# Smaller steps for GpSimd in a two-layer cross-attention kernel: weight pieces in three, a bias sum in four, stores issued later

## The chip, the core and the metric

The kernel runs on one core of one Trainium2 chip. The core has five engines that work side by side, each through its own list of instructions in order: TensorE (PE, matrix products), VectorE (DVE), ScalarE (ACT), GpSimd (POOL) and SyncE (SP, which here only issues transfers). They wait for one another through semaphores. The metric is the time of one execution on the device in microseconds (us); the median of three runs is compared.

## What is computed

Two layers of cross-attention with 16 heads of 32, all in float32. Shapes: `x` and `ctx` are 8 x 512 x 512.

```python
def L0(tgt, memory):                 # attention without a norm
    q, k, v = heads(tgt @ Wq.T), heads(memory @ Wk.T), heads(memory @ Wv.T)
    att = softmax(q @ k.T / sqrt(32)) @ v
    return tgt + att[0]              # batch 0's result is added to every batch
def L1(x, y):
    xq, ykv = layer_norm(x, gq, bq), layer_norm(y, gkv, bkv)
    q, (k, v) = heads(xq @ Wq), heads(ykv @ Wkv)
    x = x + softmax(q @ k.T * SCALE) @ v @ Wproj + bproj
    h = gelu(layer_norm(x, gm, bm) @ W1 + b1)      # 512 to 2048
    return x + h @ W2 + b2                         # 2048 to 512
```

Only `att[0]` is used, so layer 0 is worked for batch 0 alone; layer 1 for all eight batches.

## The kernel before

To keep float32 accuracy on PE, every operand is split into a rounded high part and the low rest, and a product is made of three matmuls (high x high, high x low, low x high). Making the parts is the work of ACT (high) and of DVE or POOL (low).

**Ticks.** A planner writes the order of all engines before the run. Its unit is a tick: in one tick PE makes one block of scores (128 queries x 512 keys of one head, `ps_s`, line 901), the transposed block for the softmax of seven ticks earlier (`ps_t`, 916), and the product with the values of nine ticks earlier (`ps_o`, 883), so this product follows its `ps_t` by two ticks. Between them stand parts of projections and of the MLP (`ps_d`, 862, with transposes at 792). A head is four ticks, a batch 64. The planner runs layer 0's batch first (ticks 6 to 78), then layer 1's eight batches (from tick 87), one behind the other; the MLP of batch n is worked beside the attention of the batch after it, and that of batch 8 in a tail of its own (from tick 608). Each engine goes through the ticks in the same order and does in each what the tables list for it; it waits on semaphores only, so POOL runs ahead where its inputs are there.

**What POOL does in a tick**, in this order: `p_lo` of two blocks in four (line 1285; the other two are DVE's, 1188), the joins of a group of four heads (`join`, 1256 to 1273), the norm's four small instructions (`var_e` to `shift`, 1243 to 1249), the low part of the GELU (`g_s`, 1293), low parts of whole weights, then a weight piece, an X sum (layer 0's result added to a batch of `x`, 1306), a residual sum (1320), and the bias sum. The `p_lo` of a block is needed by PE two ticks later; PE waits for it with everything behind it.

**Weight pieces.** `W1` and `W2` are split once, in 16 pieces (0 to 7 are `W1`, 8 to 15 `W2`), and written back to DRAM as high and low parts, from where the MLP loads them. `piece(i)` on POOL casts a loaded piece (`w_raw` to `piece_out`, 128 x 1024) and subtracts. Pieces 0 to 7 start at ticks 25, 30, ... 60, with load and store on SP's queue; 8 to 15 at ticks 91, 96, ... 126, on ACT's queue. The load is issued three ticks before the piece, the store two ticks (SP) or four (ACT) after. Two buffers alternate, so piece i waits until the store of piece i - 2 has landed.

**The bias sum.** After the layer norm of batch n has read `xres` (ACT, line 991), POOL adds `b2` to it, one instruction of 128 x 2048 (line 1325), at ticks 175 for batch 1, 239, 303, 367, 431, 495, 559 for batches 2 to 7, and 613 for batch 8. The MLP's second product adds to `xres` afterwards (DVE, 1119), some 30 ticks later, in the tail three ticks later. From batch 2 on, the same tick is one in which ACT makes the GELU of the batch before it in one burst, and in each of the four ticks behind it POOL has one `g_s`.

**SyncE's queue.** It issues in order the loads of heads (`q_st`, `k_st`, 707), the load of the row of maxima that each `ps_t` needs (`negmax_t`, 712), and the placing of finished heads (723, 724). The first head of a group waits until POOL's join of the group before has ended (`o_joined`, wait at 720), with all that stands behind it on the queue.

Of the kernel before, what the change touches and what calls it, by code (L numbers as in the profile page):

```python
# [5 lines left out]
F32 = mybir.dt.float32  # L6
F32R = mybir.dt.float32r
ACT = mybir.ActivationFunctionType
ALU = mybir.AluOpType
AX = mybir.AxisListType  # L10

P = 128
T = 512
D = 512
# [5 lines left out]
TC = T // P  # L20
HC = F // P
G = P // DK
# [7 lines left out]
NP = B + 1  # L30
# [191 lines left out]
def listed(pairs):  # L222
    out = {}
    for t, x in pairs:
        out.setdefault(t, []).append(x)
    return out
# [11 lines left out]
NORM_NO = {u: i for i, u in enumerate(NORMS)}  # L238
# [18 lines left out]
def ready(*u):  # L257
    return NO[u] + 1
# [8 lines left out]
def norm_ticks(kind, i):  # L267

    if kind == "y" or i and kind == "x":
        at = PLAN.end("a", (2 if kind == "y" else 10) + i, 0) - 6  # L270
        if i == 0:
            at = PRE + 1
        elif (kind, i) == ("x", 1):
            at = PLAN.gap + 3
        return (at, at, at + 1, at + 1), at + 2, (at + 3, at + 3, at + 4, at + 4)
    if kind == "x":
        at = PLAN.gap + 2
        return (at,) * 4, at, (at + 1,) * 4
    at = tuple(emptied("out", i, t) for t in range(TC))
    return at, at[-1], (at[-1] + 1,) * 4  # L280
# [46 lines left out]
PIECES = 16  # L327


def piece_tick(i):  # L330
    return PRE + 19 + 5 * i if i < PIECES // 2 else PLAN.base[1] + 4 + 5 * (i - PIECES // 2)


PIECE_SPLIT = listed([(piece_tick(i), i) for i in range(PIECES)])
X_SUMS = listed([(norm_ticks("x", b)[0][0] - (4 if b > 2 else 3) + t if b > 1 else PLAN.gap + 3, (b, t)) for b in range(1, B) for t in range(TC)])
RES_SUMS = listed([(PLAN.base[n + 1] + (4 if n == 1 else 3) + t, (n, t)) for n in range(1, NP) for t in range(TC)])
BIAS_AT = PLAN.base[2] + 2
WO_AT = PLAN.base[1] + 48
B2_SUMS = listed([(norm_ticks("h", n)[2][0] + 1, n) for n in range(1, NP)])


def sync_tables():
# [79 lines left out]
def xattn_program(nc, x, ctx, l0wq, l0wk, l0wv, wq, wk, wv, wo, w1, w2, cols, bproj, b2, ident, out):  # L422
# [179 lines left out]
    def piece_view(i, a):  # L602

        if i < PIECES // 2:
            return piece_out[:, i % 2].rearrange("p c (k a j) -> p c k a j", k=FC, a=2)[:, :, :, a]
        return piece_out[:, i % 2].rearrange("p c (a j) -> p c a j", a=2)[:, :, a]

    def piece_in(i):
        if i < PIECES // 2:
            return w1_raw[:, i % 2].rearrange("p c (k j) -> p c k j", k=FC)  # L610
        return w2_raw[:, i % 2]
# [40 lines left out]
    def load_piece(queue, i):  # L652
        if i < 2:
            queue.wait_ge(whole_split, len(WHOLE))
        elif i in (PIECES // 2, PIECES // 2 + 1):
            queue.wait_ge(unit_ready, ready("a", 10, FC - 1))
        else:
            queue.wait_ge(piece_split, i - 1)
        src = w1 if i < PIECES // 2 else w2
        c = 2 * (i % (PIECES // 2))  # L660
        queue.dma_start((w1_raw if i < PIECES // 2 else w2_raw)[:, i % 2], src[c:c + 2].rearrange("c p e -> p c e"))\
            .then_inc(piece_loaded[i % 2], 16)

    def store_piece(queue, i):
        queue.wait_ge(piece_split, i + 1)
        dst = w1d if i < PIECES // 2 else w2d
        c = 2 * (i % (PIECES // 2))
        queue.dma_start(dst[c:c + 2].rearrange("c p e -> p c e"), piece_out[:, i % 2].bitcast(F32))\
            .then_inc(piece_stored[i % 2], 16)
# [15 lines left out]
        queue.dma_start(rows(out, n - 1)[:, t], xres[n % 2][:, t]).then_inc(out_stored[n % 2], 16)  # L685

    def load_wo(queue):
        queue.wait_ge(piece_split, PIECES)
        queue.dma_start(wo_raw[:], wo).then_inc(wo_loaded, 16)


# [2 lines left out]
    def _(sp):  # L694
# [58 lines left out]
        for tick in range(TICKS):  # L753
            for h in ROWS.get(tick, []):
                load_row(h)
            early = tick < SHARED_FROM
            for u in STORES.get(tick, []) if early else ():
                store(sp, *u)
            for h in HEADS.get(tick, []):
                load_stack(h)  # L760
            for h in PLACES.get(tick, []):
                place_head(h)
            for n, g in VALUES.get(tick, []) if early else ():
                load_values(sp, n, g)
            for kind, j in LATE_W_LOADS.get(tick, []):
                load_weight(kind, j)
            for n, t in OUT_STORES.get(tick, []):
                if n == NP - 1:
                    store_out(sp, n, t)
            for kind, b in STAGE_LOADS.get(tick, []) if early else ():  # L770
                load_stage(sp, kind, b)
            if tick == PRE:
                load_stage(sp, "y", 1)
            for name, at in WHOLE_LOAD.items():
                if tick == at:
                    load_whole(name)
            for i in range(PIECES // 2):
                if tick == piece_tick(i) - 3:
                    load_piece(sp, i)
                if tick == piece_tick(i) + 2:  # L780
                    store_piece(sp, i)
        last = NP - 1
        sp.wait_ge(out_stored[last % 2], 16 * TC * (last // 2))
# [144 lines left out]
    def _(act):  # L928
# [71 lines left out]
        for tick in range(TICKS):  # L1000
# [52 lines left out]
            for i in range(PIECES // 2, PIECES):  # L1053
                if tick == piece_tick(i) - 3:
                    load_piece(act, i)
                if tick == piece_tick(i) + 4:
                    store_piece(act, i)
            if tick == WO_AT - 4:
                load_wo(act)
# [17 lines left out]
    def _(dve):  # L1077
# [4 lines left out]
        def evacuate(kind, n, c):  # L1082
            u = (kind, n, c)
            if kind == "a":
                low(u, aT[:, n % 2, 1, c], aT[:, n % 2, 0, c])
            elif kind == "ht":
                low(u, hT[:, 1, c], hT[:, 0, c])
            elif kind in ("k", "q"):
                j = KQ_NO[u] % 2
                low(u, kq_out[:, j, 1], kq_out[:, j, 0])  # L1090
            elif kind == "v":
                j = V_NO[u] % 2
                low(u, v_out[:, j, :, 1:2 * DK:2], v_out[:, j, :, 0:2 * DK:2],
                    lambda b: b.rearrange("p (h d) -> p h d", h=NH))
            elif kind == "tg":
                dve.wait_ge(unit_ready, NO[u] + 1)
                if c == 0:
                    dve.wait_ge(piece_split, PIECES // 2)
                added, own = bank(u).rearrange("p (t d) -> p t d", t=TC), slice(c * P, c * P + P)
                dve.tensor_copy(tgt2[:, :, own], added)  # L1100
                dve.tensor_tensor(xt0[:, :, own], xt0[:, :, own], added, ALU.add).then_inc(evacuated, 1)
            elif kind == "out":
                if c == 0:
                    dve.wait_ge(res_summed, n)
                dve.wait_ge(unit_ready, NO[u] + 1)
                dve.tensor_tensor(xres[n % 2][:, c], bank(u), xres[n % 2][:, c], ALU.add).then_inc(evacuated, 1)
            elif kind == "hid":
                done = GELU_NO[n, c // 4]
                if done:
                    dve.wait_ge(g_lo, 4 * done - 3 + c % 4)  # L1110
                dve.wait_ge(unit_ready, NO[u] + 1)
                dve.tensor_scalar(h_st[:, c % 4], bank(u), col_s[:, 6 * FC + c:6 * FC + c + 1], None,  # L1112
                                  ALU.add).then_inc(evacuated, 1)
            else:
                if c < TC:
                    dve.wait_ge(b2_summed, n)
                dve.wait_ge(unit_ready, NO[u] + 1)
                t = c % TC
                dve.tensor_tensor(xres[n % 2][:, t], bank(u), xres[n % 2][:, t], ALU.add).then_inc(evacuated, 1)
# [86 lines left out]
    def _(pool):  # L1206
# [5 lines left out]
            if c == FC - 1:  # L1212
                ins.then_inc(whole_split, 1)

        def piece(i):
            if i == 0:
                pool.wait_ge(unit_ready, ready("k", 0, G - 1))
            if i >= 2:
                pool.wait_ge(piece_stored[i % 2], 16 * (i // 2))
            pool.wait_ge(piece_loaded[i % 2], 16 * (i // 2 + 1))  # L1220
            pool.tensor_copy(piece_view(i, 0), piece_in(i)).then_inc(piece_hi, 1)
            pool.wait_ge(piece_hi, i + 1)
            pool.tensor_tensor(piece_view(i, 1), piece_in(i), piece_view(i, 0).bitcast(F32), ALU.subtract)\
                .then_inc(piece_split, 1)

        def split_wo(c):
            if c == 0:
# [50 lines left out]
        for tick in range(TICKS):  # L1278
# [15 lines left out]
                                   ALU.subtract).then_inc(g_lo, 1)  # L1294
            for name, c in WHOLE_LO.get(tick, []):
                whole_low(name, c)
            for i in PIECE_SPLIT.get(tick, []):
                piece(i)
            for b, t in X_SUMS.get(tick, []):
                i = STAGE_NO["x", b]  # L1300
                buf = stage[:, i % 2]
# [12 lines left out]
            for n, t in RES_SUMS.get(tick, []):  # L1314
# [5 lines left out]
                ins = pool.tensor_tensor(xres[n % 2][:, t], xres[n % 2][:, t], tgt2[:, t], ALU.add)  # L1320
                if t == TC - 1:
                    ins.then_inc(res_summed, 1)
            for n in B2_SUMS.get(tick, []):
                pool.wait_ge(normed, NORM_NO["h", n] + 1)
                pool.tensor_tensor(xres[n % 2][:], xres[n % 2][:], b2_s[:].unsqueeze(1).broadcast_to([P, TC, D]),
                                   ALU.add).then_inc(b2_summed, 1)
            for c in range(FC):
                if tick == WO_AT + 2 * c:
                    split_wo(c)
# [45 lines left out]
```

## Time and profile before

| | |
|---|---|
| median of three runs | 1836.07 us (1834.27 to 1836.93) |
| span of the profiled execution | 1833.4 us; its time outside the span is not listed |
| PE busy | 1730.2 us, 94% |
| ACT, DVE, POOL busy | 63%, 59%, 51% |
| mean granted PE clock | 0.982 of full speed |
| DMA | 354.69 MB, mean 193 GB/s |

The profile is of one execution, with times in us from the span's start. "Busy" is the time in which an engine works on an instruction; an engine can be busy half of the time and still be late where it matters. Where a row carries brackets, they hold the idle time of that engine just before the instruction and who ended it. The span and the median differ by 2.67 us, which is of the size of what is between the runs.

### The profile page before, as it was taken

To read this page: it belongs to the slowest core of one execution; us is meant where nothing else is said; L and a number is where in the kernel's file an instruction comes from. 1 tells how busy PE (TensorE), PEld (TensorE's weight loads), DVE (VectorE), ACT (ScalarE), POOL (GpSimd) and SP (SyncE) were. 2 spreads that over 40 slices of the span, in tenths; PEclk is the share of its full clock that TensorE was granted. 3 is DMA by queue.
4 is the path that set the end of the run, shared out by engine and by line. 5 is a ranking of instruction groups with operands and counts; after the bars stand their busy time and mean duration, and the time that the engine had idled before them with its cause. 6 is when DMAs were issued, how large, how long until landed. Compare 5 with 4: busy or idle time off the path is not lost.

```text
span 1833.4 us, 23939 instructions
## 1 busy us (share of the span) xinstructions
PE 1730.2 (94%) x7488; PEld 1328.0 (72%) x7488; DVE 1082.3 (59%) x1860; ACT 1156.9 (63%) x1935; POOL 933.7 (51%) x778
## 2 busy tenths in 40 slices
PE   6899998987899899999999999999999999999898
PEld 5677776765666677777777767777777777777686
DVE  4566664576776566666666665666666666564322
ACT  3677774587877675766766676667667665774231
POOL 0355531287874465466555554655556445555331
PEclk8999999999999999999999999999999999999999
DMA  6688954897645664576577556756755765567262
GB/s 233 217 295 276 301 210 153 266 319 248 209 130 166 169 196 117 167 227 181 153 216 199 139 155 188 200 130 194 231 156 159 200 189 146 162 198 243 94 215 92
DMA packets 157102, 354.69 MB, mean 193 GB/s; under 512 B 29232, under 2 KB 47792, under 8 KB 156080
## 3 DMA queue, kind: packets, MB, share of 16 engines
q1 hardware_dynamic: 101744, 174.63, 32.3%
q10 hardware_dynamic: 55232, 178.53, 30.3%
q8 instruction: 61, 1.00, 0.2%
q14 instruction: 65, 0.53, 0.1%
HBM read 251.51 MB, written 82.08 MB: 182 GB/s over the span
## 4 chain that ended last, share of the span: by engine, by line
PE 65%; ACT 10%; DVE 7%; POOL 6%; DMA 5%; issue 5%; SPq 1%; ACTq 1%; DVEq 1%; POOLq 0%
PE ps_d L862 43%; PE ps_o L883 11%; PE ps_t L916 5%; PE ps_s L901 5%; DMA q_st<-negmax_t 3%; DVE negmax L1175 1%; POOL p_lo L1285 1%; ACT p_hi L1015 1%; ACT ps_d L936 1%; POOL stage L1306 1%; ACT ps_t L1022 1%; ACT ht L991 1%; DVE stats L1132 1%; PE ps_d L792 1%; ACT h_st L1006 1%
## 5 line engine op out<-in xcount | busy, mean ns | idle before, releaser
L1285 POOL TENSOR_TENSOR p_lo<-p_full,p_hi 128x512 fp32r<-128x512 f32 x288 | 371.3, 1289 | 592.0 <-ACT p_full L1022 590.6
L1015 ACT ACTIVATE p_hi<-ps_t 128x512 fp32r<-128x512 f32 x576 | 344.8, 599 | 380.2 <-PE ps_t L916 379.5
L1175 DVE TENSOR_REDUCE negmax<-ps_s 128x1 fp32r<-128x512 f32 x576 | 389.8, 680 | 146.3 <-PE ps_s L901 145.9
L862 PE MATMUL ps_d<-hT,w_r 128*128 128x512 f32 x1536 | 421.1, 395 | 3.6 <-DVE hT L1080 1.4
L862 PE MATMUL ps_d<-w_r,g_s 128*128 128x512 f32 x1536 | 392.2, 395 | 5.6 <-DMA w_r<-w_scratch 5.6
L862 PEld LDWEIGHTS ps_d<-hT,w_r 128*128 128x128 f32 x1536 | 290.1, 189 | 75.9 <-DVE hT L1080 2.9
L862 PEld LDWEIGHTS ps_d<-w_r,g_s 128*128 128x128 f32 x1536 | 292.1, 190 | 72.1 <-issue 7.8
L1188 DVE TENSOR_TENSOR p_lo<-ps_t,p_hi 128x512 fp32r<-128x512 f32 x288 | 198.5, 689 | 235.2 <-ACT ps_t L1022 233.8
L883 PE MATMUL ps_o<-p_hi,v_s 128*65 128x512 f32 x576 | 234.7, 407 | 37.0 <-ACT o_raw L1029 27.3
L916 PE MATMUL ps_t<-q_st,k_st 97*128 97x512 f32 x576 | 233.2, 405 | 12.1 <-DMA q_st<-negmax_t 11.8
L901 PE MATMUL ps_s<-k_st,q_st 96*128 96x512 f32 x576 | 233.2, 405 | 6.7 <-DVE negmax L1175 6.6
L883 PE MATMUL ps_o<-p_lo,v_s 128*65 128x512 f32 x576 | 229.1, 398 | 0.0
L1293 POOL TENSOR_TENSOR g_s<-h_st,g_s 128x512 fp32r<-128x512 f32 x128 | 165.0, 1301 | 75.4 <-ACT g_s L1038 75.2
L1022 ACT ACTIVATE ps_t<-ps_t 128x512 f32<-128x512 f32 x288 | 172.5, 599 | 0.0
L1022 ACT ACTIVATE p_full<-ps_t 128x512 f32<-128x512 f32 x288 | 172.0, 597 | 0.0
L901 PEld LDWEIGHTS ps_s<-k_st,q_st 96*128 96x128 f32 x576 | 109.9, 191 | 53.5 <-DVE negmax L1175 12.5
L916 PEld LDWEIGHTS ps_t<-q_st,k_st 97*128 97x128 f32 x576 | 110.2, 191 | 43.3 <-DMA q_st<-negmax_t 19.0
L883 PEld LDWEIGHTS ps_o<-p_hi,v_s 128*65 128x65 f32 x576 | 79.2, 137 | 81.0 <-ACT o_raw L1029 45.0
L1112 DVE TENSOR_SCALAR h_st<-ps_d,col_s 128x512 f32<-128x512 f32 x128 | 94.2, 736 | 40.8 <-PE ps_d L862 34.8
L883 PEld LDWEIGHTS ps_o<-p_lo,v_s 128*65 128x65 f32 x576 | 79.6, 138 | 47.2 <-issue 1.6
L862 PE MATMUL ps_d<-aT,wk_s 128*128 128x512 f32 x384 | 106.7, 405 | 7.2 <-DVE aT L1080 5.7
L862 PE MATMUL ps_d<-aT,wq_s 128*128 128x512 f32 x384 | 110.3, 401 | 0.0
(99 smaller groups left out, 2166.4 us busy)
## 6 DMA issues: line engine op xcount, KB each, us to landing
w_r<-w_scratch ACTq DMA_DIRECT2D x214, 512.0 KB, 5.0
w_r<-w_scratch SPq DMA_DIRECT2D x42, 512.0 KB, 4.7
v_scratch<-v_out SPq DMA_DIRECT2D x36, 520.0 KB, 3.5
k_scratch<-kq_out SPq DMA_DIRECT2D x36, 512.0 KB, 3.7
q_st<-q_scratch SPq DMA_DIRECT2D x144, 128.0 KB, 4.5
k_st<-k_scratch SPq DMA_DIRECT2D x144, 128.0 KB, 4.3
o_ab<-o_raw SPq DMA_DIRECT2D x144, 128.0 KB, 3.7
v_s<-v_scratch ACTq DMA_DIRECT2D x31, 520.0 KB, 6.2
```

The lines of the kernel that those rows point to most:

```text
L792: ins = nc.tensor.transpose(bank(u)[:, t * P:t * P + P], src(t), id_s[:])
L862: ins = nc.tensor.matmul(bank(u), lhs[a], rhs[b], start=(i == 0 and m == 0), stop=(i == 3 and m == 2))
L883: ins = nc.tensor.matmul(ps_o[0:VW], v_s[:, group % 2, c, h % G], src[:, c], start=(c == 0 and m == 0), stop=(c == TC - 1 and m == 1))
L901: nc.tensor.matmul(ps_s[:, c % 2], q_st[0:KQ, h % G, c * P:c * P + P], k_st[0:KQ, h % G], start=True, stop=True).then_inc(s_ready, 1)
L916: nc.tensor.matmul(ps_t[:, c % 2], k_st[0:KM, h % G, c * P:c * P + P], q_st[0:KM, h % G], start=True, stop=True).then_inc(t_ready, 1)
L1015: act.activation(p_hi[:, c], ps_t[:, c % 2], ACT.Exp, scale=SCALE)
L1022: act.activation(whole, ps_t[:, c % 2], ACT.Exp, scale=SCALE).then_inc(p_exp, 1)
L1112: dve.tensor_scalar(h_st[:, c % 4], bank(u), col_s[:, 6 * FC + c:6 * FC + c + 1], None, ALU.add).then_inc(evacuated, 1)
L1175: dve.tensor_reduce(negmax[:, h % 2, c:c + 1], ps_s[:, c % 2], AX.X, ALU.max, negate=True).then_inc(s_maxed, 1)
L1188: dve.tensor_tensor(p_lo[:, c], ps_t[:, c % 2], p_hi[:, c].bitcast(F32), ALU.subtract).then_inc(p_split, 1)
L1285: pool.tensor_tensor(p_lo[:, c], p_full[:, (by_gpsimd(s) - 1) % 2], p_hi[:, c].bitcast(F32), ALU.subtract).then_inc(p_pool_split, 1)
L1293: pool.tensor_tensor(g_s[:, done % 2, 1, c], h_st[:, c], g_s[:, done % 2, 0, c].bitcast(F32), ALU.subtract).then_inc(g_lo, 1)
```

## The change

Three things. `piece(i, step)` makes of one stretch on POOL three steps, one tick each: the cast, the subtract of the first half, the subtract of the second half; counts of `piece_split` double. The stores go out two ticks later on SP's queue (tick +4) and one later on ACT's (+5). The bias sum becomes four instructions of 128 x 512, one chunk per tick, and DVE waits chunk by chunk.

```diff
-PIECE_SPLIT = listed([(piece_tick(i), i) for i in range(PIECES)])
+PIECE_SPLIT = listed([(piece_tick(i) + step, (i, step)) for i in range(PIECES) for step in range(3)])
...
-B2_SUMS = listed([(norm_ticks("h", n)[2][0] + 1, n) for n in range(1, NP)])
+B2_SUMS = listed([(norm_ticks("h", n)[2][0] + 1 + t, (n, t)) for n in range(1, NP) for t in range(TC)])
...
-            queue.wait_ge(piece_split, i - 1)
+            queue.wait_ge(piece_split, 2 * (i - 1))
...
-        queue.wait_ge(piece_split, i + 1)
+        queue.wait_ge(piece_split, 2 * (i + 1))
...
-                if tick == piece_tick(i) + 2:
+                if tick == piece_tick(i) + 4:
                     store_piece(sp, i)
...
-                if tick == piece_tick(i) + 4:
+                if tick == piece_tick(i) + 5:
                     store_piece(act, i)
...
-                    dve.wait_ge(b2_summed, n)
+                    dve.wait_ge(b2_summed, (n - 1) * TC + c + 1)
...
-        def piece(i):
-            if i == 0:
-                pool.wait_ge(unit_ready, ready("k", 0, G - 1))
-            if i >= 2:
-                pool.wait_ge(piece_stored[i % 2], 16 * (i // 2))
-            pool.wait_ge(piece_loaded[i % 2], 16 * (i // 2 + 1))
-            pool.tensor_copy(piece_view(i, 0), piece_in(i)).then_inc(piece_hi, 1)
-            pool.wait_ge(piece_hi, i + 1)
-            pool.tensor_tensor(piece_view(i, 1), piece_in(i), piece_view(i, 0).bitcast(F32), ALU.subtract)\
-                .then_inc(piece_split, 1)
+        def piece(i, step):
+            if step == 0:
+                if i == 0:
+                    pool.wait_ge(unit_ready, ready("k", 0, G - 1))
+                if i >= 2:
+                    pool.wait_ge(piece_stored[i % 2], 16 * (i // 2))
+                pool.wait_ge(piece_loaded[i % 2], 16 * (i // 2 + 1))
+                pool.tensor_copy(piece_view(i, 0), piece_in(i)).then_inc(piece_hi, 1)
+                return
+            if step == 1:
+                pool.wait_ge(piece_hi, i + 1)
+            c = step - 1
+            pool.tensor_tensor(piece_view(i, 1)[:, c], piece_in(i)[:, c], piece_view(i, 0)[:, c].bitcast(F32),
+                               ALU.subtract).then_inc(piece_split, 1)
...
-            for n in B2_SUMS.get(tick, []):
-                pool.wait_ge(normed, NORM_NO["h", n] + 1)
-                pool.tensor_tensor(xres[n % 2][:], xres[n % 2][:], b2_s[:].unsqueeze(1).broadcast_to([P, TC, D]),
-                                   ALU.add).then_inc(b2_summed, 1)
+            for n, t in B2_SUMS.get(tick, []):
+                if t == 0:
+                    pool.wait_ge(normed, NORM_NO["h", n] + 1)
+                pool.tensor_tensor(xres[n % 2][:, t], xres[n % 2][:, t], b2_s[:], ALU.add).then_inc(b2_summed, 1)
```

The lists below give an engine's instructions in order: line, operation, output<-inputs, size, and xN where N equal ones follow each other. Line numbers of the changed kernel are 4 or 5 higher here. POOL at the bias sum of batch 3 (`b_s` is `b2`, `o_ab` a join), before:

```order
L1285 TENSOR_TENSOR p_lo<-p_full,p_hi 128x512
L1325 TENSOR_TENSOR xres_b<-xres_b,b_s 128x2048
L1285 TENSOR_TENSOR p_lo<-p_full,p_hi 128x512
L1293 TENSOR_TENSOR g_s<-h_st,g_s 128x512 x2
L1285 TENSOR_TENSOR p_lo<-p_full,p_hi 128x512
L1256 TENSOR_TENSOR o_ab<-o_ab 128x512
L1293 TENSOR_TENSOR g_s<-h_st,g_s 128x512 x2
L1285 TENSOR_TENSOR p_lo<-p_full,p_hi 128x512
```

The same place after the change:

```order
L1289 TENSOR_TENSOR p_lo<-p_full,p_hi 128x512
L1330 TENSOR_TENSOR xres_b<-xres_b,b_s 128x512
L1289 TENSOR_TENSOR p_lo<-p_full,p_hi 128x512
L1297 TENSOR_TENSOR g_s<-h_st,g_s 128x512
L1330 TENSOR_TENSOR xres_b<-xres_b,b_s 128x512
L1297 TENSOR_TENSOR g_s<-h_st,g_s 128x512
L1330 TENSOR_TENSOR xres_b<-xres_b,b_s 128x512
L1289 TENSOR_TENSOR p_lo<-p_full,p_hi 128x512
L1260 TENSOR_TENSOR o_ab<-o_ab 128x512
L1297 TENSOR_TENSOR g_s<-h_st,g_s 128x512
L1330 TENSOR_TENSOR xres_b<-xres_b,b_s 128x512
L1297 TENSOR_TENSOR g_s<-h_st,g_s 128x512
```

Three of the four quarters have moved from between the first two `p_lo` to behind the second and third, among the `g_s`. POOL at piece 13, in batch 1 (`oT` and `o_ab` are the steps of a join, `var_e` to `shift` a norm), before:

```order
L1268 TENSOR_TENSOR oT<-o_ab,rs 128x512
L1243 TENSOR_TENSOR var_e<-mv,eps_s 128x4
L1244 TENSOR_SCALAR m_mean<-mv 128x4
L1246 TENSOR_TENSOR rstd<-var_e,m_half 128x4
L1249 TENSOR_TENSOR shift<-m_mean,rstd 128x4
L1221 CAST piece_out<-w_raw 128x2x512
L1223 TENSOR_TENSOR piece_out<-w_raw,piece_out 128x2x512
L1270 TENSOR_TENSOR o_ab<-o_ab,rs 128x512
L1285 TENSOR_TENSOR p_lo<-p_full,p_hi 128x512
L1273 TENSOR_TENSOR oT<-o_ab,oT 128x512
L1285 TENSOR_TENSOR p_lo<-p_full,p_hi 128x512
```

After:

```order
L1272 TENSOR_TENSOR oT<-o_ab,rs 128x512
L1247 TENSOR_TENSOR var_e<-mv,eps_s 128x4
L1248 TENSOR_SCALAR m_mean<-mv 128x4
L1250 TENSOR_TENSOR rstd<-var_e,m_half 128x4
L1253 TENSOR_TENSOR shift<-m_mean,rstd 128x4
L1222 CAST piece_out<-w_raw 128x2x512
L1274 TENSOR_TENSOR o_ab<-o_ab,rs 128x512
L1227 TENSOR_TENSOR piece_out<-w_raw,piece_out 128x512
L1289 TENSOR_TENSOR p_lo<-p_full,p_hi 128x512
L1277 TENSOR_TENSOR oT<-o_ab,oT 128x512
L1227 TENSOR_TENSOR piece_out<-w_raw,piece_out 128x512
L1289 TENSOR_TENSOR p_lo<-p_full,p_hi 128x512
```

The second half of the subtract has moved behind a `p_lo` and behind the last step of the join. ACT at the store of piece 10 (`w_scratch<-piece_out`; `stage<-x` is a load, `w_raw<-w` a piece's), before:

```order
L1022 ACTIVATE ps_t<-ps_t 128x512
L650 DMA stage<-x 128x4x512
L668 DMA w_scratch<-piece_out 128x2x1024
L991 ACTIVATE stage<-stage,shift,rstd 128x512 x2
L1015 ACTIVATE p_hi<-ps_t 128x512
L1022 ACTIVATE p_full<-ps_t 128x512
L931 ACTIVATE kq_out<-ps_d 128x512
```

After:

```order
L1022 ACTIVATE ps_t<-ps_t 128x512
L650 DMA stage<-x 128x4x512
L991 ACTIVATE stage<-stage,shift,rstd 128x512 x2
L1015 ACTIVATE p_hi<-ps_t 128x512
L1022 ACTIVATE p_full<-ps_t 128x512
L668 DMA w_scratch<-piece_out 128x2x1024
L931 ACTIVATE kq_out<-ps_d 128x512
```

The store has moved behind four of ACT's instructions, one tick nearer to the next piece's load.

## Rows read from the trace of the kernel before

**Rows 1.** The page: span, and busy us (share) of each engine.

```profile
span 1833.4 us, 23939 instructions
...
PE 1730.2 (94%) x7488; PEld 1328.0 (72%) x7488; DVE 1082.3 (59%) x1860; ACT 1156.9 (63%) x1935; POOL 933.7 (51%) x778
```

**Rows 2.** Groups of POOL's instructions: count, busy us, mean ns, idle before.

```profile
L1285 POOL TENSOR_TENSOR p_lo<-p_full,p_hi 128x512 fp32r<-128x512 f32 x288 | 371.3, 1289 | 592.0 <-ACT p_full L1022 590.6 <-DVE rs L1158 1.1
...
L1223 POOL TENSOR_TENSOR piece_out<-w_raw,piece_out 128x1024 fp32r<-128x1024 f32 x16 | 38.3, 2395 | 1.3
...
L1325 POOL TENSOR_TENSOR xres_b<-xres_b,b_s 128x2048 f32<-128x2048 f32 x4 | 18.3, 4586 | 7.2 <-ACT ht L991 7.2
```

**Rows 3.** Timeline of POOL at batch 3's bias sum: start, length.

```profile
895.51 4.60 POOL L1325 TENSOR_TENSOR xres_b<-xres_b,b_s 128x2048 f32<-128x2048 f32 x1 [1.80 <-ACT ht L991]
902.60 1.29 POOL L1285 TENSOR_TENSOR p_lo<-p_full,p_hi 128x512 fp32r<-128x512 f32 x1 [2.49 <-ACT p_full L1022]
903.86 2.55 POOL L1293 TENSOR_TENSOR g_s<-h_st,g_s 128x512 fp32r<-128x512 f32 x2
906.36 1.30 POOL L1285 TENSOR_TENSOR p_lo<-p_full,p_hi 128x512 fp32r<-128x512 f32 x1
...
908.88 1.29 POOL L1293 TENSOR_TENSOR g_s<-h_st,g_s 128x512 fp32r<-128x512 f32 x1
911.47 1.29 POOL L1293 TENSOR_TENSOR g_s<-h_st,g_s 128x512 fp32r<-128x512 f32 x1 [1.30 <-ACT g_s L1038]
912.72 1.27 POOL L1285 TENSOR_TENSOR p_lo<-p_full,p_hi 128x512 fp32r<-128x512 f32 x1
```

**Rows 4.** Timeline of PE there: products with values, high part of `p`.

```profile
901.62 0.45 PE L883 MATMUL ps_o<-p_hi,v_s 128*65 128x512 f32 x1 [2.16 <-ACT o_raw L1029]
...
910.93 0.44 PE L883 MATMUL ps_o<-p_hi,v_s 128*65 128x512 f32 x1 [0.32 <-ACT o_raw L1029]
...
915.05 0.40 PE L883 MATMUL ps_o<-p_hi,v_s 128*65 128x512 f32 x1
```

**Rows 5.** Timeline of all engines at batch 2's bias sum.

```profile
739.98 1.28 POOL L1285 TENSOR_TENSOR p_lo<-p_full,p_hi 128x512 fp32r<-128x512 f32 x1 [1.37 <-ACT p_full L1022]
...
745.15 1.29 POOL L1293 TENSOR_TENSOR g_s<-h_st,g_s 128x512 fp32r<-128x512 f32 x1 [1.37 <-ACT g_s L1038]
...
746.41 1.27 POOL L1285 TENSOR_TENSOR p_lo<-p_full,p_hi 128x512 fp32r<-128x512 f32 x1
...
748.73 0.40 PE L883 MATMUL ps_o<-p_hi,v_s 128*65 128x512 f32 x1
```

**Rows 6.** Timeline of PE behind batch 6's bias sum.

```profile
1423.08 0.50 PE L916 MATMUL ps_t<-q_st,k_st 97*128 97x512 f32 x1 [0.47 <-DMA q_st<-negmax_t]
```

**Rows 7.** Timeline of all engines at piece 6.

```profile
211.34 0.20 POOL L1243 TENSOR_TENSOR var_e<-mv,eps_s 128x4 f32<-128x4 f32 x1
...
213.10 1.52 ACT L991 ACTIVATE stage<-stage,shift,rstd 128x512 f32<-128x512 f32 x2 [0.41 <-POOL shift L1249]
...
216.71 0.96 PE L862 MATMUL ps_d<-aT,wk_s 128*128 128x512 f32 x3 [0.85 <-DVE aT L1080]
```

**Rows 8.** Waits of PE and of SP, 350 to 470 us: total, times, longest.

```profile
PE ps_t L916 <- DMA q_st<-negmax_t: 7.7, 5, 4.7
PE ps_o L883 <- POOL p_lo L1285: 4.2, 4, 1.6
...
SPq L720 <- POOL oT L1273: 3.3, 2, 3.0
```

**Rows 9.** Timeline in the second run of pieces: piece 12, and PE.

```profile
401.05 1.04 POOL L1221 CAST piece_out<-w_raw 128x1024 fp32r<-128x1024 f32 x1 [0.60 <-DMA w_raw<-w]
...
438.53 0.80 PE L916 MATMUL ps_t<-q_st,k_st 97*128 97x512 f32 x1 [4.70 <-DMA q_st<-negmax_t]
```

**Rows 10.** Busy by stretch: us; PE, PEld, DVE, ACT, POOL; PE clock, DMA, GB/s.

```profile
370.00:380.00 10.00, 9.15 (x42) 6.48 (x40) 6.58 (x11) 7.10 (x14) 9.92 (x9) 1.00 0.92 314
```

**Rows 11.** Timeline of POOL in the tail, one `g_s`.

```profile
1757.06 1.29 POOL L1293 TENSOR_TENSOR g_s<-h_st,g_s 128x512 fp32r<-128x512 f32 x1 [1.43 <-ACT g_s L1038]
```

More of the change, by code:

```diff
@@ L687, in load_wo @@
     def load_wo(queue):
-        queue.wait_ge(piece_split, PIECES)
+        queue.wait_ge(piece_split, 2 * PIECES)
         queue.dma_start(wo_raw[:], wo).then_inc(wo_loaded, 16)
@@ L1097, in evacuate @@
                 if c == 0:
-                    dve.wait_ge(piece_split, PIECES // 2)
+                    dve.wait_ge(piece_split, PIECES)
                 added, own = bank(u).rearrange("p (t d) -> p t d", t=TC), slice(c * P, c * P + P)
@@ L1296, in _ @@
                 whole_low(name, c)
-            for i in PIECE_SPLIT.get(tick, []):
-                piece(i)
+            for i, step in PIECE_SPLIT.get(tick, []):
+                piece(i, step)
             for b, t in X_SUMS.get(tick, []):
```

## The prediction

> **What bounds the kernel now.** I read the page's busy shares first. TensorE (PE) is busy for 94% of a 1833.4 us span and GpSimd (POOL) for 51% [rows 1]. So the change, which touches POOL and the queues that store its results, can move the end only where PE waits for something that POOL or those queues finish. I then took the groups of POOL's instructions for prices [rows 2], and the timeline at each place that the diff touches: the eight bias sums, and the two runs of eight pieces. What counts there is how late the next `p_lo` on POOL is against the product on PE that reads it, since PE takes its work in order.
>
> The bias sum, in batches 2 to 7, stands in a hole. In batch 3 it runs at 895.51 for 4.60 us, and POOL then idles another 2.49 us until ScalarE (ACT) has made the next `p_full` [rows 3]. PE's stall there, 2.16 us, ends on ACT's `o_raw` [rows 4], not on POOL: ACT is in its GELU. The sum costs nothing today. In the first run of pieces (100 to 230 us) one short stall touches POOL [rows 7]. In the second run (350 to 470 us) POOL matters: PE waits 4.2 us in four places for POOL's `p_lo`, and 7.7 us in five for row loads (`negmax_t`) [rows 8], of which one is 4.70 us [rows 9].
>
> **The bias in quarters.** Four instructions of the form 128x512 take 1.25 us from start to start in a row (the `p_lo` group's mean is 1.289; the two `g_s` at 903.86 give way to the next after 2.50) [rows 2, 3], against 4.59 for one of 128x2048 [rows 2]; that is 0.4 to 0.6 us more work, which alone is nothing. What counts is where they stand. The first quarter stays in the hole. The other three leave it and stand behind the next `p_lo`: one behind each of the first three `g_s`. That stretch of POOL is nearly full. In batch 3, from the `p_lo` at 902.60 to that at 912.72, it idles once, 1.30 us before the last `g_s` [rows 3]. Three more instructions are 3 x 1.25 = 3.75 us; they use up the 1.30 us, so the `p_lo` now at 912.72 starts 2.45 us later, at 915.17, and ends (1.27 us) at 916.44. Its product on PE starts today at 915.05 without waiting [rows 4]. PE will wait 916.44 - 915.05 = **1.4 us**. The `p_lo` before it goes from 906.36 to 908.86 and ends at 910.16, 0.8 us ahead of its product at 910.93 [rows 3, 4].
>
> Batches 5 and 6 repeat this pattern in the same timeline, to a tenth; 2, 4 and 7, the other three, have another. In batch 2 the same stretch has two idle times of 1.37 us, which take 2.74 of the 3.75 us; the delay is 1.01 us, and the `p_lo` that ends at 746.41 + 1.27 = 747.68 is 1.05 us ahead of its product at 748.73 [rows 5]. That costs nothing, but only by 0.04 us. In batch 6 PE waits 0.47 us a little later for a row load [rows 6] whose issue is ahead of all this, so 0.47 of its 1.4 is given back. Sum: 1.4 + 1.4 + 0.9 = **+3.7 us**. Bounds: 0, if ACT's `g_s` come later than now and POOL's idle time with them, and 6 x 1.4 = 8.4, if the other three take the fuller pattern. I take 3.7, the rows as they stand.
>
> In batch 1 no `g_s` stands beside the quarters; nothing. In batch 8, the tail, POOL waits 1.43 us for ACT before each `g_s` [rows 11] and a quarter of 1.25 us fits in; vector's additions come later still. If that cover failed, one `g_s` would be late by a fraction of a quarter.
>
> **The pieces in thirds.** A piece is now a cast (1.04) and a subtract of 2.395 us in one stretch [rows 2, 9]; it becomes 1.04 + 1.25 + 1.25 with a `p_lo` between. In the first run all `p_lo` have room. One gain: batch 5's `var_e` at 211.34 now stands behind piece 6 and started without idle time, so its input was there. With only the cast ahead it starts some 2.3 us sooner, and ACT's wait of 0.41 us for what follows from it goes. PE's stall of 0.85 us hangs on ACT there [rows 7]: **-0.4 us** (bounds -0.85 and 0).
>
> In the second run POOL is full for long stretches (9.92 of 10 us in 370 to 380 [rows 10]). In such a stretch splitting only changes the order: the first `p_lo` comes sooner, but X sums and thirds that were ahead of it come after, and the last `p_lo` ends where it ended. The gain is what is pushed past the last `p_lo` on which PE waits: one third of piece 13, 1.25 us less 0.1 for the extra instruction. The same third ends the join sooner for which SyncE waited up to 3.0 us [rows 8], and with it the 4.70 us stall; the two gains are one after the other on the same PE, so they count once, -1.15. Against it stands that piece 12 starts only when its load lands (0.60 us idle at 401.05 [rows 9]). The store of piece 10 now goes out one step later, in front of that load on ACT's queue, and may delay it by as much. I take half: **-0.5 us** (bounds -5.4, all of the 4.2 us and of one 1.2, and +3).
>
> **The stores.** SyncE's go two steps later, ACT's one, past loads of the next piece and of `stage`; vector's and the loads' new waits on the count are satisfied long before. They have no cost of their own while no row load is pushed: see the third rival.
>
> **Sum against the profiled execution:** 1833.4 + 3.7 - 0.4 - 0.5 = 1836.2 us. The median of the three runs, 1836.07, is 2.67 us above that span; I keep the distance: **1838.9 us**, 0.15% slower. A difference under 0.2% (3.67 us) can't be told from no change, so this forecast is "no difference".
>
> **Rivals.**
> *All six batches stall* (chance 0.13). For: batches 2, 4 and 7 are spared by 0.04 us [rows 5]. Against: it took two idle times in each of them. It decides at POOL's idle time in that stretch: under 2.7 us, PE waits. Price 8.4 - 0.9 = +7.5: 1843.6 us.
> *The pieces pay* (0.15). Thirds free the four `p_lo` of the second run (4.2 us) and shorten the row stall by 1.2 [rows 8], and the quarters stay covered. For: these waits are the only ones for POOL in that run. Against: the order argument above. -5.8: 1830.3 us, down to a change too small to tell if half of it comes.
> *Stores meet row loads* (0.09). Five row loads made PE wait 7.7 us, 1.5 each [rows 8], with the DMA engines busy for 0.92 of a stretch there [rows 10]. The store of piece 10 moves beside the row load of the same step, that of 15 beside another. Two more waits, +3 on top of the forecast: 1841.9 us. Against: today's stores run beside row loads too, and where both are SyncE's, the row load is issued first. The Trainium skill (DMA: Bandwidth & Descriptors, section on queues, rings and completion order) says that each DMA engine takes packets from the queues in turn; by that a store on ACT's queue would hold a row load on SyncE's queue only for its turn, and this rival would give the forecast, 1838.9; no row here separates the two.
> *Nothing shows* (0.13): the quarters find room, as in the spared batches; 1835.2 us.
>
> **How the numbers follow.** The forecast's own mechanism has 0.50; its time may be off by some 2.5 us either way, since each place is decided by tenths, so about a third of it lies above 1839.7. Slower by over 0.2%: 0.175 + 0.13 + 0.09 = 0.40. Faster: 0.12 of the second rival's 0.15. Within: the rest, 0.48. The range leaves a tenth on each side: low 1832.0 (a part of the pieces' gain), high 1844.5 (the first rival and a little).
>
> **What would show it.** After the change, PE should wait about 1.4 us for `p_lo` near 915, 1247 and 1414 us, with POOL without idle time between the two `p_lo` around it; at 748, 1081 and 1581 nothing. The stall of 0.85 us at 216.7 should halve. Waits for `p_lo` between 350 and 470 us should move rather than vanish. The prediction is wrong if the quarters find more idle time than the 1.30 us counted, if a stall there slows the matmuls behind it, as after the 4.70 us one (the next took 0.80 us, where 0.40 is usual) [rows 4, 9], or if the second run settles into another rhythm.

## The result: 0.54% slower, and the profile after

The median of 18 runs is 1845.23 us (1839.53 to 1865.90), against 1837.42 us of 18 runs of the kernel before (1832.41 to 1847.15). The ratio is 1.0054, with a 95% interval of 1.0040 to 1.0068: some 9.9 us slower (the medians differ by 7.8), where the forecast had 2.8. The median lies 0.7 us above the predicted range. Of the distance to the forecast of 1838.9, 1.35 us are the kernel before: 18 runs of it give 1837.42, where the three that the forecast started from gave 1836.07.

The page of the kernel after answers to [rows 1]: span, and busy us of the engines.

```profile
span 1852.5 us, 23979 instructions
...
PE 1739.4 (94%) x7488; PEld 1332.3 (72%) x7488; DVE 1089.2 (59%) x1860; ACT 1157.3 (62%) x1935; POOL 939.2 (51%) x818
```

POOL's groups in it answer to [rows 2]. A quarter of the bias and a third of a piece cost what was forecast (1.31 and 1.29 us); POOL has 5.5 us more work, and that alone decides nothing.

```profile
L1289 POOL TENSOR_TENSOR p_lo<-p_full,p_hi 128x512 fp32r<-128x512 f32 x288 | 371.4, 1290 | 608.8 <-ACT p_full L1022 608.6
...
L1227 POOL TENSOR_TENSOR piece_out<-w_raw,piece_out 128x512 fp32r<-128x512 f32 x32 | 41.0, 1290 | 0.5
...
L1330 POOL TENSOR_TENSOR xres_b<-xres_b,b_s 128x512 f32<-128x512 f32 x16 | 20.9, 1308 | 7.2 <-ACT ht L991 7.2
```

What PE waits for names another engine. First a line of the kernel before, then two of the kernel after (total us, times, longest). The wait for POOL's `p_lo` grew by 2.3 us from its 7.5 in the whole execution before. The wait for VectorE's (DVE's) `negmax` doubled, and its longest, 1.5 us, became 3.0.

```profile
PE ps_s L901 <- DVE negmax L1175: 6.6, 9, 1.5
```

```profile
PE ps_s L901 <- DVE negmax L1175: 13.0, 11, 3.0
PE ps_o L883 <- POOL p_lo L1289: 9.8, 10, 1.6
```

One of the two long waits is in batch 4, for which the forecast had nothing. The timeline of the kernel after there, DVE first, then POOL, then PE (start, length, engine; in brackets the idle time before, and what ended it):

```profile
1084.43 4.02 DVE L1154 COPY rs_t<-rinv 128x512 f32<-128x512 f32 x1
1088.48 0.71 DVE L1158 STREAM_TRANSPOSE rs<-rs_t 128x512 f32<-128x512 f32 x1
1089.12 1.25 DVE L1175 TENSOR_REDUCE negmax<-ps_s 128x1 fp32r<-128x512 f32 x2
```

```profile
1083.17 1.29 POOL L1297 TENSOR_TENSOR g_s<-h_st,g_s 128x512 fp32r<-128x512 f32 x1
1084.42 1.29 POOL L1330 TENSOR_TENSOR xres_a<-xres_a,b_s 128x512 f32<-128x512 f32 x1
1085.66 1.28 POOL L1297 TENSOR_TENSOR g_s<-h_st,g_s 128x512 fp32r<-128x512 f32 x1
1086.90 1.26 POOL L1289 TENSOR_TENSOR p_lo<-p_full,p_hi 128x512 fp32r<-128x512 f32 x1
1089.33 1.26 POOL L1272 TENSOR_TENSOR oT<-o_ab,rs 128x512 fp32r<-128x512 f32 x1 [1.17 <-issue]
```

```profile
1089.82 0.51 PE L901 MATMUL ps_s<-k_st,q_st 96*128 96x512 f32 x1 [3.00 <-DVE negmax L1175]
1091.02 1.65 PE L862 MATMUL ps_d<-hT,w_r 128*128 128x512 f32 x3 [0.69 <-DVE xres_b L1119]
```

DVE's copy of the inverted row sums into `rs_t` took 4.02 us. It started with a bias quarter, outlasted the `g_s` and the `p_lo` right behind it, and ended 0.29 us after the last of them. POOL then stood still because its next instruction, the join's multiplication, needs `rs`, which DVE makes from this very copy (the row names no releaser, but the code waits there for `inv_ready`, which the transposition into `rs` sets). In the kernel before, at the same place, the copy fell beside an idle time of POOL:

```profile
1077.88 0.42 DVE L1154 COPY rs_t<-rinv 128x512 f32<-128x512 f32 x1
```

```profile
1078.32 1.30 POOL L1293 TENSOR_TENSOR g_s<-h_st,g_s 128x512 fp32r<-128x512 f32 x1 [1.37 <-ACT g_s L1038]
```

To compare executions I take the starts of the `ps_t` product (one per tick) four and sixteen ticks after the bias's normalisation step: twelve ticks each, which hold the place of the loss. In us, with the duration of the copy in brackets:

| batch | before | after | bias alone | pieces alone |
|---|---|---|---|---|
| 2 | 28.02 (0.42) | 28.44 (1.55) | 28.89 (0.65) | 27.87 (0.42) |
| 3 | 27.39 (0.42) | 27.43 (0.42) | 32.31 (4.02) | 27.30 (0.42) |
| 4 | 28.11 (0.42) | 32.24 (4.02) | 30.43 (0.67) | 27.30 (0.42) |
| 5 | 27.29 (0.42) | 28.85 (0.62) | 28.42 (1.57) | 27.39 (0.42) |
| 6 | 28.02 (0.41) | 28.90 (0.67) | 28.43 (1.55) | 28.39 (0.42) |
| 7 | 27.29 (0.42) | 32.60 (4.02) | 34.97 (5.58) | 27.29 (0.42) |

After less before is 12.3 us over the six batches, 9.4 of it in batches 4 and 7, whose copies took 4.02 us. The rest of the 19.1 us between the two spans lies elsewhere: 2.7 before tick 13, ahead of all the change, and 3.4 between ticks 13 and 142. Of single executions that stretch scatters by as much: 415.5 us before, 418.9 after, and 418.2 with the old pieces, 414.1 with the new ones (the first two experiments); over the thirteen profiles (two kernels, eleven experiments) it goes from 411.8 to 418.9.

### The profile page after: what moved, and what is told of

The parts are those of the page before. It is cut to its first block, busy times and chain, and to the rows that moved or that the text cites. A ratio compares the mean times of both kernels' runs of the same rounds, so it can differ in the third digit from the quotient of the medians.

```text
span 1852.5 us, 23979 instructions
## 1 busy us (share of the span) xinstructions
PE 1739.4 (94%) x7488; PEld 1332.3 (72%) x7488; DVE 1089.2 (59%) x1860; ACT 1157.3 (62%) x1935; POOL 939.2 (51%) x818
## 4 chain that ended last, share of the span: by engine, by line
PE 69%; ACT 9%; DVE 6%; POOL 5%; DMA 5%; issue 4%; SPq 2%; ACTq 1%; DVEq 1%; POOLq 0%
PE ps_d L862 45%; PE ps_o L883 12%; PE ps_t L916 6%; PE ps_s L901 5%; DMA q_st<-negmax_t 2%; POOL p_lo L1289 1%; DVE negmax L1175 1%; ACT ht L991 1%; PE ps_d L792 1%; ACT p_hi L1015 1%; POOL stage L1310 1%; ACT ps_d L936 1%; ACT h_st L1006 1%; ACT ps_t L1022 1%; ACT L1015 1%
```

## The experiments

**Theory A:** three of the four quarters fill POOL's idle time in the stretch of `p_lo`, `g_s` and join; `p_lo` comes late, and DVE's copy, where it falls into the filled stretch, is held. **Rivals:** the pieces and stores are the loss (B); the copy is only a symptom (C); four instructions cost more than one wherever they stand (D). The runs go from splitting the change to its place, to the copy, to how long a copy is held.

**The bias alone**, on the kernel before:

```diff
-B2_SUMS = listed([(norm_ticks("h", n)[2][0] + 1, n) for n in range(1, NP)])
+B2_SUMS = listed([(norm_ticks("h", n)[2][0] + 1 + t, (n, t)) for n in range(1, NP) for t in range(TC)])
...
+                pool.tensor_tensor(xres[n % 2][:, t], xres[n % 2][:, t], b2_s[:], ALU.add).then_inc(b2_summed, 1)
```

> The kernel before with the bias add alone in four instructions on four ticks; the pieces and their stores as before. Theory A (the quarters fill the idle times of GpSimd around the bias, which makes its p_lo late by 1.4 us in batches 3, 5 and 6, and where VectorE's copy to rs_t falls beside the filled stretch, holds that copy for some 4 us instead of 0.4, for which TensorE waits 3 us and more): the whole loss is here, 7 to 11 us over the kernel before, and at least one copy to rs_t of over 2.5 us beside a quarter. Rival B (the pieces in thirds and their later stores, by which the stretch of ticks 29 to 142 ran 6 us later, are the loss): within 2 us of the kernel before.

**The pieces and stores alone**, on the kernel after, with the one add and its waits as before:

```diff
-B2_SUMS = listed([(norm_ticks("h", n)[2][0] + 1 + t, (n, t)) for n in range(1, NP) for t in range(TC)])
+B2_SUMS = listed([(norm_ticks("h", n)[2][0] + 1, n) for n in range(1, NP)])
```

> The kernel after with the bias add whole again, as before; the pieces in thirds and the later stores stay. Theory A: -2 to +2 us against the kernel before, and no copy to rs_t longer than 2 us. Rival B: 4 to 9 us over the kernel before, most of it by tick 142.

Measured: the bias alone 1.0088 (1.0058 to 1.0118), the pieces alone 0.9999 (0.9984 to 1.0013). The whole loss is the bias's; B is out. The bias alone cost some 16 us, more than the 7 to 11 expected and than the 9.9 of the whole change; the two intervals overlap, if barely. With the pieces alone no copy took over 1.55 us. With the bias alone the copy of batch 7 was held through the rest of a join instruction and four more:

```profile
1589.22 5.58 DVE L1154 COPY rs_t<-rinv 128x512 f32<-128x512 f32 x1
```

**The quarters later**, four free odd ticks, on the kernel after:

```diff
-norm_ticks("h", n)[2][0] + 1 + t
+norm_ticks("h", n)[2][0] + (9 + 2 * t if n < NP - 1 else 1 + t)
```

> The kernel after, with the four quarters of the bias on ticks +9, +11, +13 and +15 after the third normalisation step instead of +1 to +4 (batch 8 as it is): GpSimd has only p_lo there, on even ticks, and VectorE has no copy to rs_t. Theory A: the loss at the bias is gone, -2 to +2 us against the kernel before. Rival D (four instructions cost more than one wherever they stand, by their starts and by GpSimd being busy more often): 6 to 11 us over the kernel before.

**The quarters on one tick:**

```diff
-norm_ticks("h", n)[2][0] + 1 + t
+norm_ticks("h", n)[2][0] + 1
```

> The kernel after with its four bias quarters all on the first of their ticks, one behind the other in the idle time in which the kernel before has its one add of 4.60 us. Theory A (it is the place of three of the quarters, in the filled stretch beside VectorE's copy, not that there are four): -2 to +2 us against the kernel before, copies of 0.4 us at the bias in batches 2 to 7. Rival D (four instructions cost more than one wherever they stand): 4 to 10 us over it.

Measured: 0.9996 (0.9980 to 1.0011) and 1.0000 (0.9982 to 1.0018), the copies of batches 2 to 7 all at 0.42 us. The same four instructions cost nothing in either place; D is out.

**The copy as a maximum**, on the kernel after:

```diff
-                dve.tensor_copy(rs_t[:].rearrange("p (b e) -> p b e", e=DK),
-                                rinv[:].unsqueeze(2).broadcast_to([P, T // DK, DK])).then_inc(inv_copied, 1)
+                dve.tensor_reduce(rs_t[:].rearrange("p (b e) -> p b e", e=DK),
+                                  rinv[:].unsqueeze(2).unsqueeze(3).broadcast_to([P, T // DK, DK, 1]), AX.X,
+                                  ALU.max).then_inc(inv_copied, 1)
```

> The kernel after, with VectorE's copy of rinv to rs_t done as a maximum over a dimension of one element: the same numbers, an instruction that is slower by itself (an estimate of 0.6 to 0.7 us for 0.42, from the other 512-element reductions of the trace) and that does not run at the copy's double rate. Theory A with the shared port as the reason of the held copy: no such instruction over 1.5 us, the waits of 3.00 us at L901 in batches 4 and 7 are gone, the time is 3 to 5 us over the kernel before. Rival C (the copy was only late for another reason, and the lost time in batches 4 and 7 is GpSimd's own lateness): 8 to 11 us over the kernel before, with waits as long as those of the kernel after.

The same edit on the kernel before:

> The kernel before with VectorE's copy to rs_t done as a maximum over a dimension of one element. In the kernel before 22 of the 36 copies take 0.78 to 1.81 us for 0.42, and no wait of TensorE of over 1.5 us at L901 follows any. Theory A (a held copy costs only when it is held through several instructions): -2 to +1 us. Rival E (each held copy costs its excess on the path, 27.3 us less 36 times 0.68 at most): 3 us faster or more.

And with the quarters later as well:

> The kernel after with both: the quarters on ticks +9, +11, +13 and +15, and the copy as a maximum. Theory A: both take away the same loss, so together -3 to +1 us against the kernel before, like each by itself. Rival F (the two take away different losses and add up): 3 to 6 us faster than the kernel before.

Measured: 0.9993 (0.9978 to 1.0008), 1.0000 (0.9987 to 1.0014) and 0.9999 (0.9986 to 1.0013). The group of the replaced copy in the first of them:

```profile
L1154 DVE TENSOR_REDUCE rs_t<-rinv 128x512 f32<-128x512 f32 x36 | 24.4, 679 | 0.3
```

Each of the 36 takes 0.68 us, though POOL's stretch is as full as in the kernel after. So the loss needs the copy (C is out), and it is gone with either cure; both together give nothing more (F is out). E is out too: in the kernel before, a copy that waits for one POOL instruction costs nothing that shows. My expectation of 3 to 5 us over the kernel before was missed: what stays is `p_lo`, and it cost 1.2 us in batches 2 and 4 and at most 0.1 in the others (the twelve ticks took 28.71 and 28.69 against 27.5), which the times can't tell from nothing. None of these versions beats the kernel before.

**One tick further on**, so that all four quarters stand in the full stretch:

```diff
-norm_ticks("h", n)[2][0] + 1 + t
+norm_ticks("h", n)[2][0] + (2 if n < NP - 1 else 1) + t
```

> The kernel after with the four quarters one tick further on (+2 to +5; batch 8 as it is), so that all four, and not three, stand in the stretch of p_lo, g_s and join, up to the join's multiplication that waits for the copied values. Theory A, in the form that the copy is held until GpSimd itself has to wait for it: at least one more instruction to wait for, copies of over 5 us, p_lo later by up to 2.6 us, 12 to 25 us over the kernel before. Rival G (the hold is bounded, by one or by three instructions): copies of 4.1 us at most, and 6 to 12 us over the kernel before.

**The same with the copy as a maximum:**

> The kernel of the run with the quarters one tick further on, with VectorE's copy done as a maximum, so that the copy can't be held and only GpSimd's own lateness is left: four quarters of 1.29 us (5.2) against some 3.2 us of idle time before the p_lo that is waited for. Theory A with two terms: the hold, worth most of the 35 us, is gone, and p_lo is 1.2 to 2.6 us late in each of batches 2 to 7: 7 to 16 us over the kernel before, all waits of over 2 us in these places at L883 for p_lo, none at L901. Rival H (the whole 35 us came through the copy): within 3 us of the kernel before.

Measured: 1.0190 (1.0163 to 1.0216), 35 us, and 1.0059 (1.0039 to 1.0079), 11 us; so some 24 us went through the copy, and not all of the 35 (H is out). The first was expected lower (12 to 25). Its copies took 5.22 to 5.27 us in five of the six batches, which rules out a hold bounded by one or by three instructions (G). In batch 5, DVE, POOL and PE:

```profile
1261.41 5.24 DVE L1154 COPY rs_t<-rinv 128x512 f32<-128x512 f32 x1
```

```profile
1261.40 1.29 POOL L1330 TENSOR_TENSOR xres_b<-xres_b,b_s 128x512 f32<-128x512 f32 x1
1262.65 1.29 POOL L1297 TENSOR_TENSOR g_s<-h_st,g_s 128x512 fp32r<-128x512 f32 x1
1263.89 1.26 POOL L1330 TENSOR_TENSOR xres_b<-xres_b,b_s 128x512 f32<-128x512 f32 x1
1265.11 1.26 POOL L1289 TENSOR_TENSOR p_lo<-p_full,p_hi 128x512 fp32r<-128x512 f32 x1
1267.54 1.26 POOL L1272 TENSOR_TENSOR oT<-o_ab,rs 128x512 fp32r<-128x512 f32 x1 [1.16 <-issue]
```

```profile
1268.03 0.79 PE L901 MATMUL ps_s<-k_st,q_st 96*128 96x512 f32 x1 [4.22 <-DVE negmax L1175]
1269.23 1.65 PE L862 MATMUL ps_d<-hT,w_r 128*128 128x512 f32 x3 [0.40 <-DVE xres_a L1119]
```

The hold costs more than PE's wait. The twelve ticks took 34.60 us, some 7 over the 27.5 without it, for PE waits of 4.22 and 0.40: the matmuls behind ran at the lower of TensorE's two levels (1.2 GHz for 2.4), as the stretches of that kernel show (PEclk, the granted clock, is the third column from the end):

```profile
1263.00:1268.00 5.00, 0.81 (x6) 0.47 (x4) 4.97 (x4) 3.38 (x6) 3.84 (x4) 0.99 0.92 295
1268.00:1271.00 3.00, 2.57 (x5) 1.69 (x6) 2.97 (x5) 0.00 (x0) 2.04 (x2) 0.50 0.02 8
1271.00:1274.00 3.00, 3.00 (x8) 2.02 (x7) 0.78 (x2) 1.09 (x2) 1.50 (x2) 0.50 0.00 1
```

With the maximum in its place only `p_lo` is late. PE in batch 4 of that kernel:

```profile
1086.36 0.44 PE L883 MATMUL ps_o<-p_hi,v_s 128*65 128x512 f32 x1 [2.15 <-POOL p_lo L1290]
```

In batches 2, 4 and 7 the twelve ticks took 31.5 us, 4 over; in batch 4 the granted clock over the 3 us behind the wait was 0.52. In 3, 5 and 6 the wait was 0.6 us, less than the 1.2 to 2.6 expected, and the ticks took 28.35, 0.8 over, since there PE was late already (below).

**Other work in the quarters' place.** Is it the quarter's form that holds the copy, an addition in place to `xres`, or any work? On the kernel with the quarters on one tick, four idle additions per batch:

```diff
+FILL = listed([(norm_ticks("h", n)[2][0] + 2 + t, (n, t)) for n in range(2, NP - 1) for t in range(TC)])
...
+            for n, t in FILL.get(tick, []):
+                done = (n - 2) * TC + t
+                if done:
+                    pool.wait_ge(filled, done)
+                pool.tensor_tensor(bp_s[:], b2_s[:], b2_s[:], ALU.add).then_inc(filled, 1)
```

> The kernel with the four bias quarters on one tick (no loss there), plus, in batches 2 to 7 on ticks +2 to +5, one further GpSimd instruction each that adds two constants of 128x512 into a tile that nobody reads any more. It holds the places that the quarters have in the run with the quarters one tick further on. Theory A (any work of GpSimd that fills the stretch up to the join's multiplication makes p_lo late and holds the copy): copies of 4 to 5.6 us, 25 to 40 us over the kernel before. Rival I (the quarter's own form holds the copy: an addition in place into the residual that VectorE also writes): no copy over 2 us, and only p_lo late, 7 to 16 us over it as where the copy was done as a maximum.

Measured: 1.0048 (1.0022 to 1.0075), and neither theory: the time, some 9 us over, would fit rival I, but its copies don't. The copy of batch 2 was held with no quarter in the stretch:

```profile
743.20 5.83 DVE L1156 COPY rs_t<-rinv 128x512 f32<-128x512 f32 x1
```

So a hold doesn't need the quarter's form; the copies of the other batches took 0.81 to 0.84, so a full stretch is not enough. The additions took only 1.04 us each, and with that the copy met POOL at another moment. Sorting the copies by that moment gave the next theory, and its run has one operand changed:

```diff
-                pool.tensor_tensor(bp_s[:], b2_s[:], b2_s[:], ALU.add).then_inc(filled, 1)
+                pool.tensor_tensor(bp_s[:], tgt2[:, t], b2_s[:], ALU.add).then_inc(filled, 1)
```

> The kernel with the fill, whose four idle additions per batch took 1.03 us since both inputs were one tile; here one input is another tile, so that each should take 1.29 us like a quarter. So the copy should meet GpSimd at the same moment of an instruction as in the run with the quarters one tick further on. Theory A' (any instruction holds the copy, if the copy starts within some 0.2 us of that instruction's start and more stand right behind it; where it starts 0.4 us or more into it, the copy gets in at the next seam): copies of 5 us or more in at least four of batches 2 to 7, 25 to 40 us over the kernel before. Rival I (the quarter's own form holds it): at most one such copy, 7 to 16 us over it.

Measured: 1.0214 (1.0194 to 1.0235), 39 us. The copies of batches 3 to 7 took 5.25 to 5.29 us, and rival I is out. The group of the additions and a copy:

```profile
L1333 POOL TENSOR_TENSOR bp_s<-tgt,b_s 128x512 f32<-128x512 f32 x24 | 31.2, 1298 | 0.0
```

```profile
1257.13 5.29 DVE L1156 COPY rs_t<-rinv 128x512 f32<-128x512 f32 x1
```

## Why the prediction was wrong

**The step that failed** is "That costs nothing, but only by 0.04 us", for batches 2, 4 and 7, and with it the upper bound of six times 1.4 us. Its premise was "What counts there is how late the next `p_lo` on POOL is": it priced the quarters by that one thing. DVE's copy stood in the same stretch and was left out. In batches 4 and 7 it cost 4.1 and 5.3 us, three to four times what the bound allowed for a batch. That the quarters are to blame, through the copy, is shown: bias alone, pieces alone, quarters moved, copy replaced.

The trace of before held the warning, in DVE's groups:

```profile
L1154 DVE COPY rs_t<-rinv 128x512 f32<-128x512 f32 x36 | 27.3, 758 | 0.3
```

The mean is 758 ns, where an undisturbed copy takes 0.42 us; 22 of the 36 took 0.78 us or more, and each of these ran beside a POOL instruction. The Trainium skill (SBUF — State Buffer, section on who interferes with whom) states that a copy of VectorE, where it runs in a two-port mode, and an instruction of GpSimd use one pair of ports, that the one that comes second is blocked and not slowed, and that a reduction on trn2 never contends for them. The runs agree on the reduction (0.68 to 0.69 us, 36 times of 36); no row names the copy's mode. By that page the block ends with the instruction that holds the ports; here it lasted through two to four more.

**The `p_lo` term** was right in its mechanism. In batches 5 and 6 PE waits where it was forecast, for 1.14 and 1.15 us, not 1.4:

```profile
1260.17 0.45 PE L883 MATMUL ps_o<-p_hi,v_s 128*65 128x512 f32 x1 [1.14 <-POOL p_lo L1289]
...
1427.02 0.45 PE L883 MATMUL ps_o<-p_hi,v_s 128*65 128x512 f32 x1 [1.15 <-POOL p_lo L1289]
```

The twelve ticks there are 1.56 and 0.88 us longer (forecast 1.4 and 0.9, the latter with the row load's 0.47 given back [rows 6]). Batch 3 was forecast the same and lost 0.04 us. In the tail, behind batch 8, nothing was lost, as forecast: from the last `ps_t` to the end it took 151.45 us before and 151.29 after.

**The pattern of batches** (3, 5 and 6 against 2, 4 and 7) was no property of the batches. Behind PE's wait of 2.16 us for `o_raw`, the next tick took 2.32 us in batches 3, 5 and 6 of the profiled execution, and 3.37 to 3.62 in the other three. Two stretches of the kernel before, behind that wait in batches 3 and 4, show why:

```profile
901.00:904.00 3.00, 2.38 (x11) 1.79 (x12) 1.98 (x3) 3.00 (x8) 1.40 (x2) 1.00 0.68 211
1068.00:1071.00 3.00, 3.00 (x10) 2.12 (x9) 1.28 (x2) 1.89 (x4) 3.00 (x3) 0.58 0.63 175
```

After the same wait the granted clock stayed at 1.00 in one and was 0.58, mostly the lower level, in the other. Where it falls, PE itself is over 1 us late, and a late `p_lo` is hidden; that was the "idle time of 1.37". Other executions fall elsewhere: after, in batches 2, 3, 4 and 7, so that batch 3's `p_lo` cost nothing. What the clock's choice hangs on stays open.

**The pieces** came as argued. The stall of 0.85 us [rows 7] is 0.31 in the kernel after (forecast: half), as in all ten kernels with the thirds; in the three with whole pieces it is 0.85 to 0.86:

```profile
217.39 0.98 PE L862 MATMUL ps_d<-aT,wk_s 128*128 128x512 f32 x3 [0.31 <-DVE aT L1080]
```

With the pieces alone PE waits between 350 and 470 us 5.9 us for row loads and 3.2 for `p_lo`, for 7.7 and 4.2 [rows 8]; whether that is the change or scatter can't be told, since the time is the same within 0.2%. The stores cost nothing that shows either, and the rival of stores and row loads is out. "The pieces pay" and "nothing shows" fell with the loss. "All six batches stall" gave the nearest time, 1843.6, but by luck: the loss came through another engine than the one it named. The last part had asked whether "a stall there slows the matmuls behind it": it did.

## What to carry to other kernels

Before work is moved on an engine, list what the other engines run in the same stretch that shares a resource with it, not only who waits for its result; a copy whose duration varies from 0.42 to 1.81 us in one trace is such a sharer. An idle time that nobody seems to need may be the gap through which another engine gets in, and moving parts of a long instruction into that gap can cost more than the instruction. A pattern of repeats that is read from one execution is to be checked against what varies there, the granted clock first.

## What the runs showed of the hardware

How long a copy waited went with the moment at which it met POOL. I took the copies of nine kernels (all but the four in which it is a maximum) that started during a POOL instruction of 1 us or more (or up to 0.03 us ahead of it), with another right behind it. A seam is the change from one POOL instruction to the next. Of 17 copies that started within 0.2 us of that instruction's start, 14 were held until POOL's stretch had ended (4.02 to 5.83 us), three got in at the first seam (1.55 to 1.57). Of 124 that started 0.39 us into it or later, 123 got in at the next seam (1.18 us at most), and one took 5.58. What lets a copy in or keeps it out is not settled by these runs.

The granted clock has a part in that moment. Behind PE's wait for `o_raw`, over batches 2 to 7 of the thirteen profiles, it stayed at 1.00 in 26 places of 78 (the next tick took 2.32 to 2.35 us) and fell to 0.50 in 52 (3.20 to 3.88 us). With the quarters one tick further on it fell in batches 3 to 7, and the copy was held in just these; two stretches of that run, behind the wait in batches 2 and 3:

```profile
733.00:736.00 3.00, 2.96 (x13) 2.28 (x14) 2.02 (x4) 2.99 (x6) 1.97 (x2) 1.00 0.50 169
902.00:905.00 3.00, 2.91 (x8) 2.10 (x9) 1.78 (x4) 2.87 (x7) 1.92 (x2) 0.61 0.60 204
```

With the additions of two tiles it was the same. With those of 1.04 us it fell in the same five batches, and the copy was held in batch 2 alone. It is not the whole: in the kernel after the clock fell in batches 2, 3, 4 and 7, and the copy was held in 4 and 7. So where the clock falls differs from run to run, and where the copy meets POOL with it. That would fit the spread of the kernel after, 26 us from run to run for 15 before; it was not traced run by run.
